# Marks of layer 0: ScalarE copies the key rows out of PSUM, VectorE compares inside SBUF, and SyncE's late stores are spread out

## The reference, cut to what matters

```
neigh = segment_sum(edge_weight[:, None] * x[src], dst)     # row of the edge, column of its source
out   = x @ w_self + neigh @ w_neigh + bias
x     = layernorm(x + out)
```

## Time and profile before

| what | before |
|---|---|
| median of the runs | 3588.87 us |
| profiled execution, and its span | 3576.91 us, 3575.1 us |
| busy: PE, DVE, ACT, POOL | 83%, 68%, 43%, 47% of the span |
| marks on DVE (L2026), first to last start | 41.6 to 287.0 us |
| scatters on POOL (L790), first to last start | 77.3 to 581.5 us |
| pair stage on PE | 315.9 to 667 us |

### The profile page before, as it was taken

How to read it: one execution, slowest core, us unless ns; L and a number is a source line. 1 busy time by engine, 2 the same in 40 slices (tenths; PEclk the granted TensorE clock), 3 DMA queues, 4 the chain that set the end, 5 groups by cost and what they waited for, 6 DMA issues and landing times. The chain is left out here.

```text
span 3575.1 us, 59355 instructions
## 1 busy us (share of the span) xinstructions
PE 2961.2 (83%) x15273; PEld 1895.3 (53%) x15274; DVE 2435.7 (68%) x5480; ACT 1527.0 (43%) x3125; POOL 1683.7 (47%) x1731
## 2 busy tenths in 40 slices
PE   5789999989999598978769976776986569999996
PEld 2235444667777344467644434553443357587675
DVE  8895333568888898954789976569985763343444
ACT  1452222379998366631046655004654440310402
POOL 2777773046555766205777771576777300000000
PEclk6899999999999799978979997798998679999998
DMA  7998888378998365356721110993445233133241
GB/s 311 343 347 311 314 297 299 116 236 257 268 270 263 114 192 166 107 210 215 226 63 28 27 27 7 312 302 105 128 133 182 66 103 122 50 122 99 85 135 36
DMA packets 392781, 625.09 MB, mean 175 GB/s; under 512 B 129011, under 2 KB 274100, under 8 KB 385486
## 3 DMA queue, kind: packets, MB, share of 16 engines
q1 hardware_dynamic: 254085, 427.07, 36.4%
q0 software_dynamic: 72144, 145.54, 13.8%
q10 hardware_dynamic: 66365, 50.39, 4.3%
HBM read 442.67 MB, written 183.69 MB: 175 GB/s over the span
## 5 line engine op out<-in xcount | busy, mean ns | idle before, releaser
L1526 ACT ACTIVATE onehot<-iota,drel 128x128 f32<-128x128 f32 x1248 | 381.7, 388 | 684.8 <-PE ps L1231 345.1
L1231 PE MATMUL ps<-shared_sb,onehot 128*128 128x264 f32 (+1 forms) x1600 | 552.0, 441 | 93.2 <-DVE accum L2322 88.3
L2322 DVE TENSOR_TENSOR accum<-accum,ps 128x264 f32 (+1 forms) x1248 | 528.2, 423 | 10.6 <-DVE accum L2322 4.0
L1231 PEld LDWEIGHTS ps<-shared_sb,onehot 128*128 128x128 f32 x1600 | 259.4, 199 | 384.8 <-issue 239.6
L790 POOL DMA_INDIRECT t_w<-early_sb x391 | 379.6, 971 | 172.3 <-issue 94.0
L807 POOL TENSOR_SCALAR onehot<-iota,carry_d 98x512 bf16<-98x512 f32 x28 | 44.7, 1601 | 783.1 <-PE ps L1308 645.7
L1291 PE MATMUL ps<-counts_r,h_hi 128*128 128x512 f32 (+1 forms) x1050 | 322.1, 388 | 12.2 <-DVE h_lo L2584 12.2
L826 POOL DMA_INDIRECT shared_sb<-table,src_x x272 | 259.2, 953 | 115.1 <-issue 76.3
L1291 PE MATMUL ps<-counts_r,h_lo 128*128 128x512 f32 (+1 forms) x1050 | 313.0, 379 | 0.0
L826 POOL DMA_INDIRECT rows<-table,src_x x184 | 179.4, 975 | 176.5 <-DMA table<-score_sb 92.0
L873 POOL DMA_INDIRECT resid_sb<-table,src_x x224 | 211.6, 944 | 89.2 <-issue 57.7
(11 more groups left out here) (438 smaller groups left out, 6031.1 us busy)
## 6 DMA issues: line engine op xcount, KB each, us to landing
t_w<-onehot SPq DMA_DIRECT2D x13, 6400.0 KB
accum<-t_hot SPq DMA_DIRECT2D x208, 256.0 KB
shared_sb<-t_adj SPq DMA_DIRECT2D x53, 640.0 KB, 9.9
resid_sb<-t_w SPq DMA_DIRECT2D x13, 1664.0 KB
t_aside<-rows POOLq DMA_DIRECT2D x40, 512.0 KB
resid_sb<-t_w SPq DMA_DIRECT2D x13, 1536.0 KB
score_sb<-t_w SPq DMA_DIRECT2D x12, 1664.0 KB
shared_sb<-t_w SPq DMA_DIRECT2D x12, 1536.0 KB
```

What stands on the lines that cost most here:

```text
L1231: pe.matmul(ps[:, RING[(HU * h + u) % len(RING)], 0:w], onehot[:, h % 2 * HU + u, :], around[g][place(g, i, h)][:, u, 0:w], start=True, st ...
L1526: last = act.activation(onehot[:, h % 2 * HU + u, :], iota[:, 0:P], ACT.Abs, bias=drel[:, bass.ds(step + u, 1)], scale=-1.0)
L2322: dve.tensor_tensor(to, to, bank.unsqueeze(1), ALU.add).then_inc(step_acc, 1)
```

## The change

ACT now copies the key row of each of the 74 quads that DVE compares from PSUM to SBUF (`key_row`, four buffers in `resid_sb`), and DVE's four comparisons read that copy. ACT still compares every fourth quad itself, but its work is cut in two: `gaps_of(k)` in the turn of k, and `same_of(k)` after the copy of quad k+1. The bank of a quad of DVE is free for PE once it is copied, that of a quad of ACT once its four gaps are made. The six DMAs of ACT are spread over k = 16, 20, 24, 28, 32 and 36. On SP, the stores of step rows move from piece 6 of the zero fill to piece 4, and the 27 spreading DMAs are no longer issued together behind a wait for `rows_out`, but five or six behind each of pieces 7 to 11.

```diff
@@ SyncE
-                sp.wait_ge(*count("rows_out", 64))
+            def low_rows_out(these):
                 by_steps = t_lo.rearrange("n (j r) e -> (n j) r e", j=QU)
-                for i in range(S // UN + 1):
+                for i in these:
@@
-                if n == PIECES // 2:
+                if n == 4:
                     step_rows_out()
+                if n == 7:
+                    sp.wait_ge(*count("rows_out", 64))
+                if 7 <= n < 12:
+                    low_rows_out(range((S // UN + 1) * (n - 7) // 5, (S // UN + 1) * (n - 6) // 5))
@@ TensorE, keys_shown
                 if k >= 4:
-                    pe.wait_ge(*compared(k - 4))
+                    pe.wait_ge(*(count("key_used", L0H * (k // SHARE)) if on_act(k) else row_copied(k - 4)))
@@ ScalarE
+            def same_of(k):
+                if k >= SHARE:
+                    act.wait_ge(*count("quad_sum", slot_before(k) + 1))
                 act.wait_ge(*count("key_used", L0H * (k // SHARE) + L0H))
                 act.activation(same_slot(k)[:, :, :], key_gap[:, :, :], ACT.Relu, ...).then_inc(done("same_act"), 1)
...
+            def copy_row(k):
+                act.wait_ge(*count("key_ps", k + 1))
+                if k >= 4:
+                    act.wait_ge(*compared(k - 4))
+                act.activation(key_row[k % 4], ps[:, k % 4, :], ACT.Copy).then_inc(done("key_sb"), 1)
...
             for k in range(QUADS):
...
+                if not on_act(k):
+                    copy_row(k)
                 if on_act(k):
-                    compare(k)
+                    gaps_of(k)
+                if k % SHARE == 0 and k > 0:
+                    same_of(k - 1)
@@ VectorE, compare
-                dve.wait_ge(*count("key_ps", k + 1))
+                dve.wait_ge(*row_copied(k))
...
-                    last = dve.tensor_scalar(same_slot(k)[:, u, :], ps[:, k % 4, :], adj_f[...], None, ALU.is_equal)
+                    last = dve.tensor_scalar(same_slot(k)[:, u, :], key_row[k % 4], adj_f[...], None, ALU.is_equal)
```

More of the change, by code:

```diff
@@ L252, in build @@
         pick_row = over("pick_row", "resid_sb", 5120, [P])
+        key_row = [resid_sb[:, 2176 + r * EB * P:2176 + (r + 1) * EB * P] for r in range(4)]
         key_gap = flat_a[:, 4224:4224 + 2 * L0H * P].bitcast(BF16).rearrange("p (u e) -> p u e", u=L0H)
@@ L347, in build @@
                   [(f"{n}{k}", c) for k in (1, 2) for n, c in (("gat_in", NC), ("self_sub", 1), ("gat_out", NG))] + [("elu2", NC)],
-                  [("weighted1", 2), ("self_w1", 1), ("weighted2", 2), ("self_w2", 1)], [("diag_clear", 1), ("apart", S // QU), ("gaps", 3 * (S // HU))], [("x1_back", 16), ("x2_back", 16)], [("quad_sum", QUADS), ("own_mm", NT), ("adj_turned", BLOCKS * PAIRS)], [("same_act", QUADS // SHARE), ("adj_staged", BLOCKS * PAIRS)], [("w_summed", QUADS), ("own_sum", NT)], [("step_mask", EB), ("te", 1), ("adj_rows", 1), ("key_parts", 1), ("adj_ev", 1), ("keys", 2), ("pre", 1), ("attr_split", 1)], [("te_ps", 3), ("adj_tp", 1), ("steps_ps", 2), ("steps_ev", 1), ("early_one", 1)],
+                  [("weighted1", 2), ("self_w1", 1), ("weighted2", 2), ("self_w2", 1)], [("key_sb", QUADS - QUADS // SHARE), ("diag_clear", 1), ("apart", S // QU), ("gaps", 3 * (S // HU))], [("x1_back", 16), ("x2_back", 16)], [("quad_sum", QUADS), ("own_mm", NT), ("adj_turned", BLOCKS * PAIRS)], [("same_act", QUADS // SHARE), ("adj_staged", BLOCKS * PAIRS)], [("w_summed", QUADS), ("own_sum", NT)], [("step_mask", EB), ("te", 1), ("adj_rows", 1), ("key_parts", 1), ("adj_ev", 1), ("keys", 2), ("pre", 1), ("attr_split", 1)], [("te_ps", 3), ("adj_tp", 1), ("steps_ps", 2), ("steps_ev", 1), ("early_one", 1)],
                   [("p0_" + n, c) for n, c in parts], [("rest_" + n, c) for n, c in in_three],
@@ L412, in compared, with row_copied @@
             return count("same_act", k // SHARE + 1) if on_act(k) else count("same_dve", k - k // SHARE + 1)
+        def row_copied(k):
+            return count("key_sb", k - k // SHARE + 1)
         def same_slot(k):
@@ L1424, in _, with gaps_of @@
                 act.sem_inc(hot_kept[h], 16)
-            def compare(k):
+            def gaps_of(k):
                 act.wait_ge(*count("key_ps", k + 1))
                 if k >= SHARE:
-                    act.wait_ge(*count("quad_sum", slot_before(k) + 1))
                     act.wait_ge(*count("same_act", k // SHARE))
@@ L1449, in _ @@
+            def copy_row(k):
[3 more added lines that the diff above has]
+                act.activation(key_row[k % 4], ps[:, k % 4, :], ACT.Copy).then_inc(done("key_sb"), 1)
             for k in range(QUADS):
                 if k == 16:
-                    first_loads()
+                    act.wait_ge(*count("attr_split", 1))
+                    act.wait_ge(*count("adj_ev", 1))
+                    act.dma_start(t_attr.rearrange("(b q) e -> q b e", b=SB), attr_b.rearrange("p b m e -> p b (m e)")).then_inc(done("attr_out"), 16)
+                elif k == 20:
+                    act.dma_start(rows[:, :, :], a["rows"]).then_inc(done("ld_rows"), 16)
+                elif k == 24:
+                    act.dma_start(vecs[:, :, :], a["vecs"]).then_inc(done("ld_vecs"), 16)
+                elif k == 28:
+                    act.dma_start(weights[:, :, 0:D], a["L0_gnn_weight"].rearrange("(c p) n -> p c n", p=P)).then_inc(done("ld_w0"), 16)
+                elif k == 32:
+                    act.dma_start(cols[:, :, :], a["x_cols"].rearrange("(c p) n -> p c n", p=P)).then_inc(done("ld_x"), 16)
+                elif k == 36:
+                    act.dma_start(hrows[:, :, 0:D], a["x_pad"].rearrange("(t p) d -> p t d", p=P)).then_inc(done("ld_xh"), 16)
+                if not on_act(k):
+                    copy_row(k)
@@ L2025, in compare @@
                 for u in range(L0H):
-                    last = dve.tensor_scalar(same_slot(k)[:, u, :], ps[:, k % 4, :], adj_f[:, k * L0H + u:k * L0H + u + 1], None, ALU.is_equal)
+                    last = dve.tensor_scalar(same_slot(k)[:, u, :], key_row[k % 4], adj_f[:, k * L0H + u:k * L0H + u + 1], None, ALU.is_equal)
                 last.then_inc(done("same_dve"), 1)
```

## The result

The changed kernel takes 3597.65 us (median of 20 runs, 3590.59 to 3604.59), the kernel before 3585.86 us (20 runs beside them). The ratio is 1.0033 with a 95% interval of 1.0024 to 1.0042: slower by 11.8 us (8.6 to 15.1), where the forecast had 22.7. One execution of the kernel before took 9114.15 us and is left out of the ratio. The profiled execution took 3597.71 us with a span of 3595.9.

What follows compares the result with a forecast made beforehand. DVE's marks and the zero fill, then PE in the pair stage, bound the kernel, with POOL a third chain. Start 11.4 us earlier, POOL's 39 us delay beyond 4.9 us slack: +22.7 on 3588.87, 3611.6 us; range 3577 to 3658.

Steps and rivals of the forecast that it cites:

- the sum X - 16.3: Pair stage's end: start 11.4 us earlier, POOL's delay beyond 4.9 us of slack added; +22.7 us with a delay of 39.
- POOL's delay X: POOL's scatters beside comparisons inside SBUF fall 39 us behind by 240 us; forecast range 24 to 60.
- the slack of 16.3 us: Before pair 11's load at 602.35: POOL's last scatter, with 3.6 us for landing, is done at 586.
- Comparisons at 0.48 us: DVE's 296 comparisons fall from 729 ns to 0.48 us when read from SBUF, saving 74 us of DVE time.
- A round of 6.5 to 7 us: Marks: a round of four quads falls from 8.4 us, no longer bound by DVE; marks end at about 240.
- The earlier marks are covered by the fill: Before the pair stage: marks ending 40 to 55 us earlier gain nearly nothing alone, since loads wait for the zero fill.
- The price of 0.40 us for each scatter: POOL beside SBUF comparisons: 0.40 us added to each of 98 scatters from 77 to 240 us, 39 us in all.
- the shut-out rival: POOL is shut out for whole rows of comparisons: delay of 60 to 100 us, 80 gives +64, 3653 us; chance 0.2.
- The gather of 22.84 us: POOL beside a short SBUF pass: a gather taking 1.13 us, its extra 0.17 us put down to L1913.
- the one of 6.52 us: POOL's gather that stood 6.52 us beside 32 short passes in a row, the evidence for whole-row shut-out.
- Break-even: POOL's delay at which the change neither gains nor loses: 16.3 us, or 0.11 us per scatter.
- The start does not enter the sum: Pair stage: the 11.4 us gained at PE's start shrink POOL's slack to 4.9 us, so POOL takes them at the end.

Runs made afterwards that it cites:

- experiment 2: The changed kernel with SyncE's stores put back as before; 3595.03 us, ratio 1.0040 to the kernel before.
- 3: The changed kernel with DVE's comparisons reading PSUM again, ACT's copies kept; 3575.64 us, ratio 0.9975 to the kernel before.
- variant 9: The kernel before with SyncE's stores spread, ACT comparing every third quad and its six DMAs spread over quads 16 to 36; 3572.79 us, ratio 0.9963.
- 4: The kernel before with SyncE's stores spread and ACT comparing every third quad, no copies; 3575.17 us, ratio 0.9983.
- experiment 1: The kernel before with only SyncE's stores moved and spread; 3581.12 us, ratio 0.9997.
- variant 8: The changed kernel with DVE waiting for its own last pass between quads and between the four comparisons; 3571.17 us, ratio 0.9957 to the kernel before.
- 10: The changed kernel with DVE waiting between quads and between comparisons, but SyncE's stores as before; 3579.01 us, ratio 0.9986 to the kernel before.

## Why the prediction was wrong, step by step

The direction and the chain held: comparisons inside SBUF delay POOL's scatters, the last of these delays pair 11, and the stage ends later (experiments 2 and 3). The rise was forecast at 22.7 us and came at 11.8 by the medians, 12.8 by the means of two profiles each. The failed step is the size of **the sum X - 16.3**. POOL's delay X was put too large, and the slack of 16.3 us, which is taken off it, too small, so both errors raise the forecast.

- *Comparisons at 0.48 us.* 0.47 to 0.48. A round of 6.5 to 7 us: 6.6, and bound by PE. Marks ended at 226 instead of 240; the spread DMAs of ACT, which were not counted as a gain there, may be most of that (they brought 15.5 us in variant 9 against 4).
- *The earlier marks are covered by the fill.* Right: 52 us of idle PE before 304.49. The first load was forecast at 295 and PE's start at 304.5; they came at 293.90 and 304.49. The stores alone paid nothing (experiment 1); beside earlier marks and a free POOL they did (8 against 10).
- *X, POOL's delay.* Forecast 39 us; the last scatter came 36.2 us later in the first pair of profiles, and 33.0 on the mean of both (615.75 less 582.75). The price of 0.40 us for each scatter was too low (42.6 us of loss on 84 of them is 0.51) and the number of 98 too high, since the marks ended 14 us sooner than forecast. Less the 4.7 us that 112 scatters lose before, the loss is 37.9 us in the first pair of profiles, and 33.5 in the second, beside the forecast 39: that this came so near is luck, as the two errors nearly cancel. The price was also put together from delays of single passes, and those are small: 41 scatters lost 0.2 us each. Most of the delay comes from what I had given to the shut-out rival with a chance of 0.2, scatters that wait out a whole row of passes. That rival was right for rows of eight and wrong for rows of four, which let a scatter in after the third pass, and so far too large in size; rows of eight come only about once in 8 quads.
- *Rows read too simply.* The gather of 22.84 us, read as 0.17 us beside L1913, ran until 23.97 and so also beside L1914, a pass with two inputs (23.15 to 23.84): it does not price a single short pass. And before the one of 6.52 us, two gathers (1189.49 and 1190.78) took 0.98 and 1.01 us beside the same row of 32 passes, which starts at 1189.30; the long one ended 0.8 us after that row. So already before, a row shut out some scatters and not others. Break-even is 0.14 us per scatter by the prediction's own formula (116 scatters of 1.27 + 0.14 us in 163 us), not 0.11.
- *The slack of 16.3 us.* It is 19.9. I had allowed 3.6 us for the last scatter's landing; the changed kernel shows 1.4 (618.6 to 619.97, and 612.9 to 614.30). That is 2.2 us. The other 1.4 us come from taking the need from one execution: pair 11's load goes out at 602.35 there and at 605.70 in the second, the last scatter's end at 582.4 and 583.1.
- *The sum.* With the measured terms, each the mean of two profiles, it is 33.0 - 19.9 = 13.1 us; from that load to the end of the stage it is 64.4 us on the mean, and 64.7 before, so 12.8 us, beside 11.8 by the medians. So of the 9.9 us between 22.7 and 12.8, 6.0 are X, 3.6 the slack and 0.3 the last pairs. The forecast time of 3612 us is too high by another 3 us, since it stood on a base of 3588.87 us from three runs, and twenty gave 3585.86.
- *The start does not enter the sum.* Right (experiment 2).

The change thus does three things: the closed hole and the spread ACT DMAs let the stage start earlier, the marks end earlier still and that is covered by the fill, and back-to-back SBUF passes cost POOL more than its slack.

The stage ends at 662.4, 666.4 and 658.2 us in variants 3, 8 and 9, although all start it within 1 us of each other. The traces place the 8.2 us between variants 8 and 9: 0.7 at the start, 3.6 in PE's idle times (13.7 against 10.1 us, counting those over 0.3 us), and 4.0 in matmuls that took longer together. From 580 to 590 us, in which PE first stood idle for 4.71 us, the granted clock is 0.70 in variant 8, where it is 1.00 in variant 9; from 306 to 400 us it is 0.97 against 0.99. Why PE's loads come later in one execution than in the other stays open.

Open too is what follows the stage: between 2905 and 2917 us in all profiles, with the same code. For single variants this is as large as the differences between them, so that their order is known by the medians alone and not explained. Which end of a pass lets a waiting scatter in is not known either. A version of variant 8 with fewer pauses (one after the second pass) was not tried.

## What to carry to other kernels

Before an operand is moved from PSUM to SBUF to speed DVE up, look at which indirect DMAs POOL issues beside it and how much slack that chain has at its far end; and if it has little, let DVE wait for its own result between the passes where it has time to spare. A gain on an engine counts only when the next gate (here the zero fill) is moved in the same change, and moving that gate alone brought nothing here: test such parts singly and together. A slack of a few us read from one execution is no firmer than that execution; read it from two.

## What the runs showed of the hardware

- A comparison of 128x512 (one fp32 source, bf16 out) took 0.73 us from PSUM and 0.47 to 0.48 us from SBUF, at a pace of 0.40 us when four follow each other.
- A scatter (0.96 us alone) that begins 0.13 to 0.16 us before a row of eight such SBUF passes took 3.49 to 3.53 us in nine cases, until 0.12 to 0.13 us after the eighth. One that begins when a quad has just started took 1.22 to 1.26 us and was over 0.12 to 0.15 us after the third pass, with the fourth running. Beside comparisons that read PSUM it takes 0.96 us.
- With a wait for completion after each pass the same passes, at 0.50 us and 91% load, cost POOL next to nothing: the mean from 100 to 180 us is 0.96 us, where it is 1.4 us in the changed kernel. The waits lengthen a round of 12 passes by 1.1 us against the changed kernel (7.7 for 6.6 us).
- An issue of DMAs with small pieces can hold a queue long: `t_drel` held SyncE for 28.82 us at piece 4 of the fill and for 26.79 us at piece 6 in the kernel before. Pieces of the fill were in flight, and the DMA share stayed at 1.01 from 78 to 107 us. The 27 spreading DMAs took 0.67 us each to issue with the DMA engines partly idle (18.07 us in all), and the first five of them 6.2 us each among the fill (31.11 us).
